# Self-attention on one Trainium2 core: softmax probabilities normalised on VectorE ahead of their transposes

## What is computed

```python
q = (x @ Wq.T).reshape(B, S, N_HEADS, HEAD_DIM).transpose(0, 2, 1, 3)
k = (x @ Wk.T).reshape(B, S, N_HEADS, HEAD_DIM).transpose(0, 2, 1, 3)
v = (x @ Wv.T).reshape(B, S, N_HEADS, HEAD_DIM).transpose(0, 2, 1, 3)
q = _apply_rope(q)
k = _apply_rope(k)
scores = jnp.einsum('bhqd,bhkd->bhqk', q, k) / np.sqrt(HEAD_DIM).astype(np.float32)
scores = jnp.where(causal, scores, -jnp.inf)
attn = jax.nn.softmax(scores, axis=-1)
out = jnp.einsum('bhqk,bhkd->bhqd', attn, v)
out = out.transpose(0, 2, 1, 3).reshape(B, S, N_HEADS * HEAD_DIM)
return out @ Wo.T
...
x = _layernorm(x + _L0_attn_ref(x, L0_attn_Wq, L0_attn_Wk, L0_attn_Wv, L0_attn_Wo), axis=-1)
```

## Time and profile before

| | us |
|---|---|
| median of 3 timed runs | 1959.2 (1956.88 to 1959.33) |
| profiled execution, whole | 1966.56 |
| profiled execution, span of the trace | 1964.7 |
| self-attention in it, from the start to the last store | 0 to 638.8 |

### The profile page before, as it was taken

One profiled execution on the slowest core, in us unless ns is written; L12 is line 12 of the kernel. 1 busy time (PEld: TensorE's weight loads), 2 busy tenths in 40 slices (PEclk: granted clock), 3 DMA queues, 4 the chain that ended last, 5 costly groups with the idle time before them and its releaser, 6 DMA issues. The chain is left out here.

```text
span 1964.7 us, 40878 instructions
## 1 busy us (share of the span) xinstructions
PE 1684.6 (86%) x11428; PEld 922.5 (47%) x11492; DVE 1421.5 (72%) x1915; ACT 1378.4 (70%) x2861; POOL 849.0 (43%) x1378
## 2 busy tenths in 40 slices
PE   5999999999994699999999999998336777777776
PEld 4877777777773233333333333333113333333332
DVE  3555555555553788888888888887448999999986
ACT  4555555555552378787777777786529999999996
POOL 3466566556553322323223232232364554545542
PEclk8999999999997699999999999998558888888887
DMA  3333433433433554444444443444233333333311
GB/s 113 102 102 112 127 105 113 124 109 110 123 116 104 119 167 117 107 108 106 105 115 110 107 107 105 114 111 147 80 88 94 109 99 97 109 99 112 96 65 43
DMA packets 118563, 210.97 MB, mean 107 GB/s; under 512 B 32097, under 2 KB 34689, under 8 KB 116737
## 3 DMA queue, kind: packets, MB, share of 16 engines
q1 hardware_dynamic: 110338, 209.51, 37.5%
q0 software_dynamic: 8192, 1.07, 0.3%
HBM read 133.41 MB, written 76.02 MB: 107 GB/s over the span
## 5 line engine op out<-in xcount | busy, mean ns | idle before, releaser
L926 DVE TENSOR_REDUCE b_smax<-b_m 128x2 f32<-128x1024 f32 x512 | 602.7, 1221 | 111.6 <-PE b_m L981 109.9
L901 ACT ACTIVATE b_prob<-b_e 128x512 f32<-128x512 f32 x1024 | 528.1, 603 | 138.5 <-PE b_e L1017 138.4
L1017 PE MATMUL b_e<-b_xs,b_cs 50*128 50x512 f32 x1024 | 358.8, 477 | 19.6 <-DMA b_xs<-b_max_part 5.6
L1017 PEld LDWEIGHTS b_e<-b_xs,b_cs 50*128 50x128 f32 x1024 | 143.9, 187 | 305.9 <-ACT b_prob L901 274.5
L1002 PE MATMUL b_av<-b_prob,b_vT 128*32 128x512 f32 x2048 | 278.5, 617 | 0.0
L1775 PE MATMUL c_y_ps<-c_w,c_hqT 128*128 128x512 bf16 x481 | 175.8, 532 | 112.3 <-issue 104.5
L981 PE MATMUL b_m<-b_cs,b_xs 48*128 48x512 f32 x1024 | 236.1, 434 | 37.1 <-DMA b_gamma<-in_gamma 30.9
L852 POOL TENSOR_SCALAR b_max_part<-b_neg_max 16x128 fp32r<-16x128 f32 x64 | 18.4, 288 | 464.6 <-ACT b_neg_max L892 464.6
L362 ACT ACTIVATE a_prob<-a_bank,a_neg_max 128x128 f32<-128x128 f32 x512 | 179.5, 386 | 54.7 <-DVE a_neg_max L442 54.7
L1775 PEld LDWEIGHTS c_y_ps<-c_w,c_hqT 128*128 128x128 bf16 x512 | 64.0, 129 | 214.0 <-issue 190.9
L862 POOL DMA_DIRECT2D b_xs<-b_max_part x256 | 136.0, 537 | 43.7 <-POOL b_max_part L855 36.9
(11 more groups left out here) (149 smaller groups left out, 3142.3 us busy)
## 6 DMA issues: line engine op xcount, KB each, us to landing
scratch_c_part<-a_c_part SPq DMA_DIRECT2D x64, 256.0 KB
scratch_x_part<-a_x_part SPq DMA_DIRECT2D x64, 256.0 KB
b_xs<-scratch_x_part SPq DMA_DIRECT2D x128, 128.0 KB, 3.0
b_cs<-scratch_c_part SPq DMA_DIRECT2D x128, 128.0 KB, 3.0
scratch_heads<-b_heads SPq DMA_DIRECT2D x64, 256.0 KB, 2.4
a_xT<-in_xT SPq DMA_DIRECT2D x32, 256.0 KB, 5.1
a_c_in<-in_ctx SPq DMA_DIRECT2D x32, 256.0 KB, 2.6
a_x<-in_x SPq DMA_DIRECT2D x32, 256.0 KB, 5.3
```

The source lines that it names most:

```text
L901: act.activation(prob[k % 8][:, :], e_ps[bank_of(k)][:, :], ACT.Exp, scale=0.25).then_inc(exp_done, 1)
L926: dve.tensor_reduce(smax[g][:, :, j, qc], m_ps[u % 2][:, :, :], AX.X, ALU.max, negate=True).then_inc(max_done, 1)
L1017: pe.matmul(e_ps[bank_of(2 * u + e)][:, :], cs[p][g][half(e), j, lc * P:(lc + 1) * P], xs[p][g][half(e), j, :], start=True, stop=True).the ...
```

## The change

The division by the row sums moves from after the product with V to before the transposes of the probabilities. For each of the four banks VectorE takes the reciprocals of its four row sums (128x4) and multiplies the 128x512 block of `prob` with them in place, both operands in SBUF. TensorE's `spread`, ScalarE's `spread_out` and VectorE's one multiplication of `o_ps` are gone, and with them the tiles `rdenT` and `oT`: `out_high` and `out_low` read `o_ps` in PSUM. The four engines' `step` functions are written in another order, and TensorE's and ScalarE's pipelines are two steps deep instead of one (VectorE's three instead of two; SP stores one step later).

```diff
-            def denominators(b):
-                dve.wait_ge(exp_done, 4 * b + 4)
-                if later(b):
-                    dve.wait_ge(spread_done, b)
-                dve.reciprocal(rden[:, :, :], den[:, :, :].rearrange("p j c -> p c j")).then_inc(rden_done, 1)
+            def normalise(b, j):
+
+                dve.wait_ge(exp_done, 4 * b + j + 1)
+                dve.reciprocal(rden[:, j, :], den[:, j, :]).then_inc(rden_done, 1)
+                dve.wait_ge(rden_done, 4 * b + j + 1)
+                dve.tensor_tensor(prob[:, j, :, :], prob[:, j, :, :], rden[:, j, :].unsqueeze(2).broadcast_to([P, KC, P]),
+                                  ALU.mult).then_inc(norm_done, 1)
...
             def transpose_prob(b, j):
-                pe.wait_ge(exp_done, 4 * b + j + 1)
+                pe.wait_ge(norm_done, 4 * b + j + 1)
...
             def step(t, on):
+                if on(1):
+                    values(t - 1)
+                    exponentials(t - 1, 0)
+                    exponentials(t - 1, 1)
                 if on(0):
                     query(t)
                 if on(1):
+                    exponentials(t - 1, 2)
                     exponentials(t - 1, 3)
-                    values(t - 1)
+                if on(2):
+                    out_high(t - 2)
+                if on(0):
+                    k_transposed(t)
+                if on(1):
                     prob_transposed(t - 1, 0)
-                    prob_transposed(t - 1, 2)
-                    spread_out(t - 1)
+                    prob_transposed(t - 1, 1)
                 if on(0):
                     q_transposed(t)
...
```

More of the change, by code:

```diff
@@ L231, in _ @@
             load_weight(3, "woT")
-            for t in range(1, 5):
+            for t in range(1, 6):
                 step(t, lambda k: k <= t)
-            with sp.Fori(5, NB) as t:
+            with sp.Fori(6, NB) as t:
                 step(t, lambda k: True)
-            for t in range(NB, NB + 4):
+            for t in range(NB, NB + 5):
                 step(t, lambda k: t - k < NB)
@@ L391, in step @@
                 if on(1):
+                    exponentials(t - 1, 2)
                     exponentials(t - 1, 3)
-                    values(t - 1)
+                if on(2):
+                    out_high(t - 2)
+                if on(0):
+                    k_transposed(t)
+                if on(1):
                     prob_transposed(t - 1, 0)
-                    prob_transposed(t - 1, 2)
-                    spread_out(t - 1)
+                    prob_transposed(t - 1, 1)
                 if on(0):
                     q_transposed(t)
[L399 to L406, removed]
+            pipeline(act, NB, 2, step)
         @block.vector
@@ L480, in prob_transposed @@
                     pT_dve, 1)
[L482 to L489, removed]
-            def step(t, on):
+            def step(t, on):
+                if on(1):
+                    maxima(t - 1, 1)
+                    maxima(t - 1, 2)
+                    maxima(t - 1, 3)
+                    normalise(t - 1, 0)
+                    normalise(t - 1, 1)
+                if on(0):
+                    rope_k(t)
+                if on(1):
+                    normalise(t - 1, 2)
+                    normalise(t - 1, 3)
+                if on(2):
+                    out_low(t - 2)
+                if on(1):
+                    prob_transposed(t - 1, 2)
+                if on(3):
+                    norm_x1(t - 3)
+                if on(1):
+                    prob_transposed(t - 1, 3)
                 if on(2):
@@ L575, in transpose_prob, with attend @@
                 last.then_inc(prob_tr, 1)
-            def spread(b):
-                pe.wait_ge(rden_done, b + 1)
+            def attend(b):
                 pe.wait_ge(v_done, b + 1)
-                for c in range(KC):
-                    for j in range(HPC):
-                        last = pe.matmul(v_ps[DH * j:DH * (j + 1), c * P:(c + 1) * P],
-                                         rden[:, c, j:j + 1].broadcast_to([P, DH]), ident[:, :],
-                                         start=True, stop=True)
-                last.then_inc(spread_done, 1)
-            def attend(b):
                 pe.wait_ge(pT_act, 2 * b + 2)
@@ L609, in step @@
                     project(t, 0)
+                    project(t, 1)
+                    project(t, 2)
                 if on(1):
                     transpose_prob(t - 1, 0)
+                if on(0):
+                    transpose_k(t)
+                if on(1):
                     transpose_prob(t - 1, 1)
[L613 to L615 removed]
                     transpose_prob(t - 1, 2)
[L617 to L618 removed]
                 if on(0):
                     transpose_q(t)
[L621 removed]
+                if on(1):
+                    transpose_prob(t - 1, 3)
+                if on(2):
+                    out_projection(t - 2)
+                if on(0):
+                    scores(t)
                 if on(1):
                     attend(t - 1)
[L624 to L628 removed]
             pe.wait_ge(const_ld, 16 * CONSTS)
[L631 removed]
+            pipeline(pe, NB, 2, step)
 def cross_attention(nc, NB, t_in, scratch, ffn_stage, ffn_abs):
```

75 lines of the change are left out of this document (17 added, 58 removed).

## The result

The changed kernel takes 1948.55 us (median of 20 runs, 1941.57 to 1956.77), the kernel before 1967.49 (20 runs, 1956.88 to 1968.86). The ratio of the runs is 0.9921 [0.9908, 0.9933], about 15.5 us less, and the two medians lie 18.9 us apart, where the forecast was 33.5 less. The sign is as forecast, and 1948.55 lies inside the range of 1911 to 1951, but only about half of the gain came, and the time is outside the likeliest case's own 1918 to 1937.

What follows compares the result with a forecast made beforehand. TensorE bounds the kernel: a step of 18.27 - 1.01 - 0.29 = 16.97 us, with a 0.35 us stall and 0.1 for gaps 17.4; with the ends, 1959.2 - 33.5 = 1925.7 us, range 1911 to 1951.

Steps and rivals of the forecast that it cites:

- likeliest case: The forecast's own case for self-attention: a step of 17.15 to 17.75 us, total 1918 to 1937 us, chance 0.55.
- the floor: Shortest new step from TensorE's own work: 18.27 less 1.01 for the spreading and 0.29 for xT's wait, 16.97 us.
- The chain of K's rotation, banks 2 and 3 and the low part: VectorE's work between V's projection and the output projection: ends at 5.35 us unhindered, with GpSimd stalls TensorE 0.35 us.
- the timetable: VectorE and GpSimd instructions placed from V's projection as 0, each excluding the other; output projection at 6.2 us.
- floor of 5.84: TensorE's time from V's projection to the output projection: 2.64 for a projection plus 3.20 for transposes, 5.84 us.
- releases read from the earlier trace: VectorE's two-SBUF-operand instructions and GpSimd each wait until the other lets go, about 0.15 us ahead of its recorded end.
- the start of Q's sines: GpSimd begins Q's rotation 0.24 us after ScalarE's copy of Q, at -0.85 us counted from V's projection.
- What else is late: Other waits in a step (residual, probT's copy, Q's transposes, power, SP's queue of loads and stores), all costed at nothing.
- The tail: From the last scores to the block's end: three stores of 7.9, 7.9 and 5.9 us from 17.5 on, 39.2 us.
- Longer products: Rival: VectorE's products take 0.85 to 1.0 us by in-place writes or broadcast; step 17.8 to 18.3, 1938 to 1954 us, chance 0.15.
- GpSimd in front of bank 3: Rival: the context's subtraction on GpSimd precedes bank 3's product; output projection at 7.55, step 18.7, total 1966 us, chance 0.1.
- No stall: Rival: VectorE's products wait less for GpSimd and the chain ends at 5.35; step 16.97, total 1912.4 us, chance 0.2.

Runs made afterwards that it cites:

- r3: The changed kernel with x_part's store issued ahead of the context's load and K's cosine product kept in PSUM: 1916.64 us, 0.9762 of the kernel before.
- r5: The changed kernel with its four products replaced by maxima with one operand in PSUM, so no division by the row sums: 1908.23 us (one run).
- r1: The changed kernel with SyncE issuing x_part's store ahead of the context's load: 1927.67 us, 0.9828 of the kernel before.
- r6: r1 with ScalarE copying Q ahead of bank 1's exponentials: 1966.63 us (one run), steady step 18.67 us.
- r7: r3 repeated unchanged in the second series for its profile: 1916.55 us (one run), steady step 16.87 us.
- r8: r3 with separate x1 and x_part buffers for the last three batches: 1905.18 us, 0.9711 of the kernel before.
- r2: The changed kernel with K's cosine product kept in PSUM, so K's last addition has one SBUF operand: 1939.54 us, 0.9872 of the kernel before.

## Why the prediction was right and wrong

**Right.** Where nothing else takes longer, as in r3 to r5, a step is bound by TensorE and loses what leaves it. The spreading and the wait for xT are gone, VectorE's residual waits for TensorE and no longer for x, and with nothing in the way the step is 16.79 us where I had taken 16.97 as the floor. The chain of K's rotation, banks 2 and 3 and the low part is the one that stalls, by the exclusion of a VectorE instruction with two SBUF operands and GpSimd. In r1, where GpSimd is on time, the timetable holds: K's addition 0.69, bank 2's product long by its wait, the output projection at 5.93 (6.2 forecast), the step 17.25 (17.4). Two misses cancel there in part: GpSimd started 0.27 us earlier than forecast (-1.12), and the rest of the step, from the output projection to the next V projection, takes 11.32 us (17.25 - 5.93) where the forecast's pieces give 11.13 (16.97 - 5.84). The floor of 5.84 itself was too long. In r5, with nothing in the way, it is 5.46 (318.02 to 323.48): the six transposes were put at 3.20 and take 2.73 (320.75 to 323.48). By that floor the changed kernel stalls 1.19 us in each step, which is the 0.80, 0.16 and 0.24 us ahead of its weight loads, and its step of 18.0 is 1.21 above r5's. The releases read from the earlier trace rows hold too. Bank 2's product of 1.56 us did its own 0.69 from 321.91 on, and Q's sum is recorded to 322.04, 0.13 us later. On this the Trainium skill ("SBUF — State Buffer", Who interferes with whom) says that the second of the two blocks fully until the first has finished; the trace agrees, with 0.69 against up to 1.80 us for the same product.

**Wrong: the placing of GpSimd.** The step of the argument is the start of Q's sines, "GpSimd starts 0.24 later (315.78 to 316.02) at -0.85". It took for granted that GpSimd is idle by then, as it was before (4.03 us of waiting in the earlier trace rows). In "What else is late" I followed x in SP's queue, noted that the stores queue behind it, and costed all of it at nothing. I didn't follow x_part: its store stands behind the context's load in the queue, the context waits for its split, the store's landing is 6.6 us later (325.54 to 332.11), and with the new order on GpSimd, x1's split stands ahead of the power and of Q's rotation. The sines came at -0.25 and 0.5 us was added to each step (17.92 against 17.4), 16 us in all. What set the step is the circle told below r5, 10.57 us of GpSimd and 7.43 of queue and landing, which the forecast never added up. The prediction's marker of a step over 18 was touched (18.0 steady), but it named no mechanism that would lead there. TensorE's waits are for VectorE, as forecast, 0.80 us where 0.2 to 0.7 was: GpSimd holds it up only through VectorE.

**Wrong: the exclusion was looked for only in the chain.** The products of banks 0 and 1 "are long ready" for TensorE, and so I didn't ask whom they hold up. They hold up GpSimd's split and power (1.61 and 1.01 us instead of 1.29 and 0.55), as r5 shows.

**The tail, +2.9.** Splits from the last scores on were forecast at 25.4 and 33.3 us and the end at 39.2; they came at 26.2, 34.2 and 42.1. 0.9 us of the miss is at the splits; 2.0 are the last store, to which I gave its landing only (5.9) and not the split ahead of it (7.93 from 615.74 on).

**The rivals.** Longer products gives the right size (17.8 to 18.3) for a wrong reason: the products take 691 ns whenever nothing excludes them. GpSimd in front of bank 3 didn't happen in this kernel, and its price was right: it said 18.7, and r6, where it does happen together with Q's sum in front of K's addition, has 18.67. That is luck in part, since r6 has a second wait that the rival didn't have, and the output projection comes at 7.33 and not at 7.55. No stall was called 16.97 and is 16.79 to 16.87, reached by r3 to r5, r7 and r8.

**What stays open.** In r2 the store takes 6.9 us from issue to landing against 6.65 in the changed kernel, without a cause here. Whether GpSimd made earlier would cost or gain, with VectorE left as it is, wasn't tried. Whether GpSimd's order alone (the power and Q's rotation ahead of x1's split) would do as well as moving the store wasn't tried. The 10 us by which the code behind the block differs from trace to trace has no cause here; its short cases go with a higher mean clock (0.92 and over, against 0.915 to 0.918).

## What to carry to other kernels

When a change reorders an engine, walk each in-order queue with it, the DMA queue too, and ask of each store not only who waits for its data but who waits for its buffer: 6.6 us of landing behind a queued load took half the gain here. Then add up the circle that the buffer closes, since no step can be shorter. An engine that excludes another has to be placed for the whole step, not only in the chain that stalls, since a delay starts where the cover is thick and arrives where it is thin. An instruction that must run beside GpSimd is best given a PSUM operand (K's addition from a median of 1445 to 691 ns in r2, the step from 17.25 to 16.86 beside the moved store).

## What the runs showed that I had not expected

- The recorded duration holds the wait. The same product of 128x512 is shown with 691 to 1801 ns, with no idle time ahead of it, so VectorE's 78.7 of 100 us busy is partly waiting: without the second SBUF operand it is 73.2 for as many instructions in a shorter step.
- Of two instructions that exclude each other the one that starts 0.06 us earlier runs and the other waits its whole length (r6). K's addition, ready 0.33 us later than in r1, turned that order round, and the step went from 17.25 to 18.67 us.
- A reciprocal of 128x4 takes 0.16 to 0.18 us and the dependent product starts 0.03 to 0.04 us behind it; I had taken 0.20 and 0.04.
- Taking the waits away from stores moved the limit to their issue and landing: SP takes 1.5 us for the two x_part stores of a steady step and 3.06 for the same two when the stores crowd.
